# GpSimd adds all eight key tiles of a unit, and TensorE sums one tile with a product of ones instead of three

## What is computed

```
x: 4 x 1024 x 256, four heads of 64
h = layernorm(x) * (1 + ca) + sa
q, k, v = heads(layernorm(h) @ w.T)          # q and k normalised by their rms
sim  = q @ k.T                               # per batch and head, 1024 x 1024
attn = softmax(sim, axis=-1)                 # exp(sim - max) / sum(exp(sim - max))
out  = attn @ v                              # then the output projection, times ga, plus x
```

## Time and profile before

| | us |
|---|---|
| median of three executions | 2362.71 |
| their range | 2361.69 to 2371.12 |
| the profiled execution, its own time | 2366.97 |
| span in its trace | 2365.1 |

### The profile page before, as it was taken

How to read it: one execution, slowest core, us unless ns; L and a number is a source line. 1 busy time by engine, 2 the same in 40 slices (tenths; PEclk the granted TensorE clock), 3 DMA queues, 4 the chain that set the end, 5 groups by cost and what they waited for, 6 DMA issues and landing times.

```text
span 2365.1 us, 36446 instructions
## 1 busy us (share of the span) xinstructions
PE 1967.3 (83%) x12941; PEld 1407.0 (59%) x12941; DVE 1479.5 (63%) x3723; ACT 1189.5 (50%) x2717; POOL 1029.9 (44%) x788
## 2 busy tenths in 40 slices
PE   4569999998836889888888888876888888888887
PEld 3444454444424767667676766755676666757666
DVE  3678887777436557475674755664665756657474
ACT  0545556343325455554555555553645555455553
POOL 0314556464634344443443435443544435344452
PEclk6679999999957999999999998988999999999999
DMA  4000000110140000000000002010000000000000
GB/s 132 32 16 25 10 23 27 34 33 29 49 139 5 11 22 14 20 14 15 20 16 19 14 16 63 12 55 24 23 20 25 21 25 23 17 28 22 27 15 22
DMA packets 83406, 68.57 MB, mean 29 GB/s; under 512 B 10853, under 2 KB 79509, under 8 KB 83225
## 3 DMA queue, kind: packets, MB, share of 16 engines
q1 hardware_dynamic: 83224, 66.25, 9.2%
HBM read 45.22 MB, written 16.81 MB: 26 GB/s over the span
## 4 chain that ended last, share of the span: by engine, by line
PE 39%; DVE 14%; issue 6%; ACT 6%; DMA 5%; SPq 1%; POOL 0%; DVEq 0%; ACTq 0%; POOLq 0%
PE bank_A L1170 5%; PE bank_P L259 5%; PE bank_O L1193 5%; PE bank_T L1181 4%; PE bank_P L261 4%; PE bank_P L260 4%; DMA l_xs<-l_xs 4%; PE bank_T L1160 3%; PE bank_A L259 2%; PE bank_A L261 2%; PE bank_A L260 2%; ACT l_sm L1327 2%; DVE l_sm L1512 2%; ACT l_pt L1336 1%; DVE l_ra L91 1%
## 5 line engine op out<-in xcount | busy, mean ns | idle before, releaser
L1705 POOL TENSOR_TENSOR l_sm<-l_sm,l_rinv 128x512 f32<-128x512 f32 (+1 forms) x256 | 284.1, 1114 | 327.8 <-DVE l_rinv L1520 327.7
L1327 ACT ACTIVATE l_sm<-l_sm,l_nb 128x256 f32<-128x256 f32 (+1 forms) x512 | 249.0, 487 | 205.2 <-DVE l_nb L1512 204.8
L1512 DVE CUSTOM_DVE_ANT_0 l_sm<-bank_A,l_mask 128x256 f32<-128x256 f32 (+1 forms) x512 | 187.3, 402 | 232.8 <-PE bank_A L1170 232.1
L1693 POOL TENSOR_TENSOR l_t<-l_qk,l_tab 128x512 f32<-128x512 f32 x128 | 170.2, 1351 | 360.2 <-DVE l_ss L1479 328.5
L259 PE MATMUL bank_A<-l_f_hi,l_w_hi 128*114 128x256 f32 (+1 forms) x768 | 222.3, 289 | 3.5 <-DVE l_f_lo L1553 2.4
L1170 PE MATMUL bank_A<-l_kt,l_qt 64*128 64x256 f32 (+1 forms) x1024 | 184.4, 439 | 44.7 <-DVE l_nb L1512 44.7
L261 PE MATMUL bank_A<-l_f_hi,l_w_lo 128*114 128x256 f32 (+1 forms) x768 | 216.5, 282 | 0.0
L260 PE MATMUL bank_A<-l_f_lo,l_w_hi 128*114 128x256 f32 (+1 forms) x768 | 216.3, 282 | 0.0
L259 PE MATMUL bank_P<-l_wqkv_hi,l_h_hi 128*128 128x512 f32 x384 | 167.6, 436 | 54.3 <-ACT l_qk L1299 32.3
L1193 PE MATMUL bank_O<-l_pt,l_vt 128*64 128x128 f32 x1920 | 165.9, 290 | 48.0 <-DVE l_o_lo L1524 36.9
L1336 ACT COPY l_pt<-bank_T 128x512 f32<-128x512 f32 (+1 forms) x256 | 139.1, 543 | 132.5 <-PE bank_T L1181 132.5
(11 more groups left out here) (242 smaller groups left out, 5107.4 us busy)
## 6 DMA issues: line engine op xcount, KB each, us to landing
l_xs<-x_layers SPq DMA_DIRECT2D x64, 128.0 KB, 2.5
x<-in_x SPq DMA_DIRECT2D x8, 512.0 KB, 3.9
base_rows<-x SPq DMA_DIRECT2D x16, 256.0 KB, 2.1
x_layers<-x SPq DMA_DIRECT2D x16, 256.0 KB, 2.2
l_xs<-x_layers SPq DMA_DIRECT2D x64, 64.0 KB, 2.2
x_layers<-l_yb SPq DMA_DIRECT2D x32, 128.0 KB, 1.8
l_base<-base_rows SPq DMA_DIRECT2D x32, 128.0 KB, 2.6
out<-l_yb SPq DMA_DIRECT2D x32, 128.0 KB, 1.7
```

What stands on the lines that cost most here:

```text
L1327: eng.activation(row, row, ACT.Exp, bias=nb[:, R % SS, e:e + 1], scale=-1.0, accum_out=rsum[:, R % SS, e:e + 1]).then_inc(ex_ready, 1)
L1512: eng.tensor_tensor_reduce(sm[:, R % SS, e, 0:P * windows(n)], ps[:, 0:P * windows(n)], keep, 1.0, 3.0e38, ALU.add, ALU.min, nb[:, R % SS, ...
L1693: eng.tensor_tensor(dst[:, :, :, lo:lo + H2], src[:, :, :, hi:hi + H2], table[:, :, 1, lo:lo + H2].unsqueeze(2).to_broadcast([P, 2, LH, H2 ...
L1705: eng.tensor_tensor(row, row, rinv[:, R % SS, :].unsqueeze(2).to_broadcast([P, 2, P * windows(n)]), ALU.mult).then_inc(pn_ready, 1)
```

## The change

GpSimd adds for kt = 1 to 7 instead of 1 to 5: seven adds for each unit instead of five. `row_sums` multiplies only `acc` by the ones: two calls of `matmul` instead of six, one for each half. It waits for the seventh add of its unit. The exponentials that overwrite tiles 6 and 7 wait for their adds instead of the row sums. Nothing else is edited; lines below the edit have numbers lower by 3 (TensorE) or 6 (GpSimd).

```diff
             def row_sums(U):
                 fill(t, "r", U, "M")
-                R = NT * U
-                for i, part in enumerate((pr[:, (R + 6) % A_PR], pr[:, (R + 7) % A_PR], acc)):
-                    if i == 2:
-                        t.wait_ge(acc_done, 5 * (U + 1))
-                    for e in range(2):
-                        last = eng.matmul(M[HD * e:HD * e + HD, 0, :], one[:, :], part[:, e, :], start=(i == 0), stop=(i == 2))
+                t.wait_ge(acc_done, (NT - 1) * (U + 1))
+                for e in range(2):
+                    last = eng.matmul(M[HD * e:HD * e + HD, 0, :], one[:, :], acc[:, e, :], start=True, stop=True)
                 last.then_inc(done["r"], 1)
...
                     t.wait_ge(pv_done, R - A_PR + 1)
-                    if kt < 6:
-                        t.wait_ge(acc_done, 5 * U + max(kt, 1))
-                    else:
-                        t.wait_ge(done["r"], U + 1)
+                    t.wait_ge(acc_done, (NT - 1) * U + max(kt, 1))
...
             for n, j, R in ticks():
-                if 0 <= R < A_RUNS and 1 <= R % NT < 6:
+                if 0 <= R < A_RUNS and R % NT >= 1:
```

## The result

The changed kernel takes 2378.38 us, the kernel before 2365.09 us in the same sets of runs (medians of 15 each). The ratio is 1.0055, 95% interval 1.0042 to 1.0068: 13.0 us, or 0.55%, slower. My forecast of 2366 was within half a per cent of no change; the time came out just above the upper end of the range, 2378. The profiled execution of after took 2375.13 us, that of before 2366.97, which is 8.2 us.

The account below looks back on a forecast made before the run. TensorE was taken to set the pace, VectorE close behind. Terms -23.9 + 10.3 + 5.8 + 11.4 - 1.3 gave +2.3, plus 1 for the clock +3.3 us, so 2366 us against the median; range 2352 to 2378, 8 in 10.

Parts of the forecast that it names:

- 14 units x 1.71: Units 0 to 13: TensorE's queue loses the products of tiles 6 and 7, 1.71 us per unit, 23.9 us gained.
- six chains: Stages 4 to 8 and 10: VectorE's small chain instructions wait out GpSimd's seventh add, 10.3 us lost, reaching TensorE in full.
- unit 11: Stage 9: GpSimd is full, adds of unit 10 push its queue and VectorE waits longer for `xr`; 5.8 us lost.
- units 14 and 15: End of the stretch: GpSimd's queue runs to 644.3, so the last sums end at 645.4 instead of 634.0; 11.4 us lost.
- tail behind the last sums: A stage behind the last sums: VectorE's work that waited for `xr` is over before the sums come; 1.3 us back.
- clock at the end: TensorE may fall to its lower clock level earlier during the longer end stall; up to 1.5 us, 1 added.
- upper bound of 15 us: Most that the chains could lose: 6 x 2.5 us; the lower bound was 0, with the chain ahead each time.
- The rival in which VectorE wins the ports: Chains start ahead of the seventh add or delays vanish in a later wait; -8.0 us, 2355 us; chance 0.17.
- The first add waits: Sign in the profile after: GpSimd's first add of a unit waits about 60 us in total instead of 128.
- The lead at unit 10: Sign: kernel 8 to 12 us ahead up to unit 10; near 19 (no ports) or under 5 (more collisions) refutes.
- the clean gain: Rival: GpSimd's waits of 128.5 us hold all 81 us of new adds; 27.4 us gained, 2335 us; chance 0.05.
- GpSimd as the bound in more stages: Rival, stages 7, 9 and 11: GpSimd instructions stretch beside VectorE's, 12 us over three units, 2378 us; chance 0.16.

Follow-up runs that it names:

- e1: Kernel before with the row-sum products of tiles 6 and 7 removed and no GpSimd adds added, so both tiles are missing from the sums; 2341.8 us, ratio 0.9899.
- e6: Kernel before with one more VectorE reduction of 2.29 us, result unused, in the chain of stages 4 to 8 and 10; 2387.37 us, ratio 1.0089.
- e9: Kernel before with the additional VectorE reduction of e6, plus ten unused TensorE products filling the idle time ahead of the maxima; 2385.99 us, ratio 1.0086 to the kernel before.
- e3: The changed kernel, but units 11, 14 and 15 keep five adds and three products; 2368.19 us, ratio 1.0014 to the kernel before.
- e2: Kernel before with seven GpSimd adds per unit while TensorE keeps its products, so tiles 6 and 7 count twice; 2403.02 us, ratio 1.0160.
- e5: The changed kernel, with GpSimd waiting for the end of VectorE's chain before the seventh add in stages 4 to 8 and 10; 2363.51 us, ratio 0.9997 to before.
- e7: The changed kernel with eight unused TensorE products filling the idle time behind each chain, ahead of the maxima; 2380.11 us, ratio 1.0059 to the kernel before.

## Why the prediction came out wrong

The mechanisms were the right ones and stood in the right places. The sum was +3.3 us and the attention stretch grew by 12.1. Term by term, forecast against measured:

| term | forecast | measured |
|---|---|---|
| 14 units x 1.71 | -23.9 | -23.9 (e1: about 1.71 each) |
| six chains | +10.3 | +17.6 (port waits 12.0, the clock behind them 5.6) |
| unit 11 | +5.8 | +7.4 |
| units 8 and 12 | 0 | +1.1 |
| units 14 and 15 | +11.4 | +12.3 |
| tail behind the last sums | -1.3 | -0.7 |
| clock at the end | +1 | within the line above |
| slower start in before's profile | not in the sum | -1.8 |
| sum | +3.3 | +12.0, of 12.1 |

- **The step that failed** is "Sum 10.3 us for six chains". It priced the port waits alone. These came near: 12.0 us measured, with stages 4 to 7 within about 0.2 us of the forecast and 0.9 and 0.8 too low in stages 8 and 10. But the forecast followed the delay to TensorE's wait and stopped there, as if the stretch behind ran on unchanged. TensorE then stood idle for 1.8 to 3.5 us, and behind five of the six stalls it ran at about half its clock, which leaves 5.6 us over the port waits. e6 and e9 show it by itself: a stall of 2.29 us costs 3.4 to 3.9, and 2.27 to 2.30 at three places where the clock stays up. e3 and e2 show it with the change's own stalls. The upper bound of 15 us was wrong for the same reason, and it made the range too narrow. I had used the clock only for the longer stall at the end, with 1 us.
- A part of the miss is not the change's: 2366 stood on the 2362.71 of three executions, and fifteen of the same kernel have 2365.09. Against that the forecast was +3.3 us and the measurement +13.0.
- The Trainium skill's page "SBUF — State Buffer", section "Who interferes with whom", says that order of issue decides who blocks, since whichever comes first holds the pair for the whole instruction. The trace agrees, with 2.39 us for L716, started 0.04 us behind the add, against 0.17 to 0.19 for its like. All that were hit are TENSOR_SCALAR with one tensor as input, not the kind with two SBUF inputs that the prediction took from the page; for these the prediction had L88 of the earlier trace rows. e5 agrees as well: with the chain first, the loss is gone. The rival in which VectorE wins the ports is this e5. It doesn't happen by itself but had to be arranged with a wait.
- **Unit 11** was 1.6 us too low: VectorE waits 9.20 us for `xr`, not "near 7". The two adds of unit 10 push GpSimd's queue by more than I let them: measured from the sums of unit 10, the first add of unit 11 starts 3.6 us later than before, where I had reckoned 2.0 (512.7 against 510.7). In e3, with unit 11 itself unchanged, 4.6 us are lost to them.
- **The end** was right in kind and nearly in size: 12.34 us of waiting against "some 10", 12.3 lost against 11.4. The list of work there is written as 31.1 us from 608.2; 31.1 is what follows 613.2, from 608.2 it adds up to 36.1, and the 644.3 is right. The 1 us for the clock at the end rests on no row, and no run takes it apart from the rest.
- **The tests I had named.** The first add waits 64.3 us ("about 60"), and small instructions of `roots` take 1.3 to 2.4 us in six stages. The lead at unit 10 was 6.3 us where I had named 8 to 12; and 1.8 of the 6.3 comes from before's slower start. The 4.5 that remain are under the 5 that I had named as proof of more collisions. They stood at no more places: two chains were hit twice, and each place but the first cost more than its port wait.
- Of the rivals, the clean gain fell with the last row sums, and "GpSimd as the bound in more stages" gave the number, 2378, but not the cause: units 8 and 12 lost 0.5 and 0.6 us, and e5, with the same work on GpSimd, loses 0.5 at unit 7 and 0.8 at unit 13.

What stays open: why the clock fell behind 1.77 us of idling in stage 6 and not behind 1.76 in stage 4, nor behind the 2.86 us of e3; why the excess is no larger in stages 5 and 7 (0.8 and 1.0 us), whose windows show the longer slow stretch, than in stages 6, 8 and 10 (1.4, 1.5 and 0.9); why the fillers of e7 and e9 held the clock in some stages only; and why their shorter stretches don't show in the timed runs.

## What to carry to other kernels

A spare engine's average room says little. Ask what is short and urgent on VectorE while the new GpSimd work runs, and let the engine with room wait for the urgent one: one wait on GpSimd turned +13 into -1 us, and leaving out four crowded units turned that into -17.5. When a delay reaches a TensorE that is otherwise nearly always busy, price the stall and also the products behind it at the lower clock; here each stall of 2 to 3 us behind which the clock fell cost about one more. And where a queue is full, work added to the unit ahead counts too: of the 7.4 us of unit 11, 4.6 came with unit 11 itself unchanged.

## What the runs showed of the hardware

- A small instruction of VectorE (8 to 48 columns, 0.17 to 0.21 us alone) that meets a GpSimd add of 2.4 us took up to 2.39 us: it waited for the end of the add.
- An idle TensorE pays twice. In a stretch of 94% busy at clock 1.00, five of the change's six idle gaps of 1.8 to 3.5 us were followed by windows with a mean of 0.52 to 0.67. Over all kernels the excess was 0.8 to 1.7 us for each gap behind which the clock fell, with one misfit of 0.2 in e9. The length of the gap alone didn't decide it: 1.76 us was followed by a fall in e2 and 2.86 us by none in e3.
- The layers' part is the same instructions in every kernel, yet it lasts 1692 to 1703 us from profile to profile. The two windows of it, before and e1:

```profile
670.00:2365.00 1695.00, 1429.02 (x10048) 1117.56 (x10048) 1015.11 (x2949) 896.29 (x2295) 728.25 (x592) 0.95 0.08 25
```

```profile
645.00:2348.00 1703.00, 1437.23 (x10048) 1126.33 (x10048) 1015.25 (x2949) 895.31 (x2295) 727.63 (x592) 0.94 0.08 25
```

PE is busy for 8.2 us longer with the same 10048 products, at a mean clock of 0.94 instead of 0.95, while DVE, ACT and POOL agree within 1 us. Effects of a few microseconds in the attention stretch drown in this, which is why the small steps here are read from the stretch and not from the total.
